# One pass instead of two over the second layer norm of an eight-core state-space and mixture-of-experts kernel

## What is computed

```python
def _layernorm(x, axis=-1, eps=1e-5):
    m = jnp.mean(x, axis=axis, keepdims=True)
    v = jnp.var(x, axis=axis, keepdims=True)
    return (x - m) / jnp.sqrt(v + eps)

x = L0_attn_x                                   # (4, 4096, 1024)
x = x + _L0_attn_ref(_layernorm(x), ...)        # a state-space scan per feature, then W_out
x = x + _L0_ffn_ref(_layernorm(x), ...)         # the second layer norm, router, 16 experts, shared MLP
return x
```

## Time and profile before

| what | us |
|---|---|
| median of the 2 timed runs | 9272.08 |
| the two runs | 8994.34 and 9549.82 |
| the profiled execution | 8383.0 |
| its span, core 2, the slowest | 8381.4 |
| spans of the 8 cores | 8336.9 to 8381.4 |
| TensorE busy in the span | 7658.5 (91%) |
| VectorE busy | 1614.3 (19%) |
| ScalarE busy | 662.4 (8%) |
| second layer norm, statistics pass | 1831.8 to 1879.4 |
| second layer norm, normalising pass | 1879.4 to 1930.8 |

### The profile page before, as it was taken

One profiled execution on the slowest core, in us unless ns is written; L12 is line 12 of the kernel. 1 busy time (PEld: TensorE's weight loads), 2 busy tenths in 40 slices (PEclk: granted clock), 3 DMA queues, 4 the chain that ended last, 5 costly groups with the idle time before them and its releaser, 6 DMA issues.

```text
span 8381.4 us, 128676 instructions; the slowest of 8 cores (8336.9 to 8381.4 us)
## 1 busy us (share of the span) xinstructions
PE 7658.5 (91%) x56312; PEld 6610.2 (79%) x56312; DVE 1614.3 (19%) x3078; ACT 662.4 (8%) x1195; POOL 479.2 (6%) x334
## 2 busy tenths in 40 slices
PE   0688888936999999999999997999999999999998
PEld 0688888424888888888888885888888888888886
DVE  5333333022111111111111111111111111111111
ACT  3211111011000000000000000000000000000000
POOL 0343433000000000000000000000000000000000
PEclk9655555967999999999999998999999999999998
DMA  2000000032011100110010102001110010100111
GB/s 81 15 3 3 3 3 5 20 123 66 31 36 45 41 31 31 51 41 31 31 49 33 41 31 71 31 31 35 46 41 31 31 51 31 41 31 31 51 41 41
DMA packets 129946, 309.18 MB, mean 37 GB/s; under 512 B 18384, under 2 KB 19408, under 8 KB 129392
## 3 DMA queue, kind: packets, MB, share of 16 engines
q1 hardware_dynamic: 124784, 284.17, 9.6%
q10 hardware_dynamic: 3456, 12.58, 0.5%
q0 software_dynamic: 1152, 4.19, 0.2%
HBM read 284.11 MB, written 16.78 MB: 36 GB/s over the span
## 4 chain that ended last, share of the span: by engine, by line
PE 88%; DVE 4%; POOL 2%; DMA 2%; issue 2%; ACT 1%; SPq 0%; DVEq 0%; POOLq 0%; ACTq 0%
PE ps L110 88%; POOL R L110 2%; DVE R L110 1%; ACT R L110 1%; DVE STA L110 1%; DMA SCA<-x1sp 1%; DVE SCB L110 1%; DMA SCA<-xo 1%; SPq L110 0%; DMA x1sp<-SCB 0%; DVE gsc L110 0%; DMA out<-SCB 0%; DVEq L110 0%; DVE hsb L110 0%; DMA R<-ws 0%
## 5 line engine op out<-in xcount | busy, mean ns | idle before, releaser
L110 PE MATMUL ps<-R 128*128 128x256 f32 (+3 forms) x33024 | 4976.8, 336 | 80.4 <-ACT R L110 33.3
L110 PEld LDWEIGHTS ps<-R 128*128 128x128 f32 (+1 forms) x33024 | 4330.8, 198 | 681.1 <-issue 169.3
L110 PE MATMUL ps<-SCA,R 128*128 128x256 f32 (+1 forms) x8704 | 1350.3, 328 | 4.8 <-DVE R L110 4.8
L110 PEld LDWEIGHTS ps<-SCA,R 128*128 128x128 f32 (+1 forms) x8704 | 1182.9, 200 | 135.2 <-issue 15.5
L110 PE MATMUL ps<-hsb,R 128*128 128x256 f32 x4608 | 1021.7, 382 | 0.0
L110 PEld LDWEIGHTS ps<-hsb,R 128*128 128x128 f32 x4608 | 878.9, 191 | 129.4 <-issue 9.3
L110 ACT ACTIVATE SCA<-ps,bcol 128x256 f32<-128x256 f32 x576 | 272.8, 474 | 5489.1 <-PE ps L110 5446.5
L110 DVE TENSOR_TENSOR R<-R,ps 128x256 f32<-128x256 f32 x1088 | 458.2, 421 | 953.3 <-PE ps L110 865.9
L110 PE MATMUL ps<-KE,R 128*128 128x128 f32 (+1 forms) x944 | 203.7, 396 | 468.7 <-POOL R L110 322.8
L110 PEld LDWEIGHTS ps<-KE,R 128*128 128x128 f32 (+1 forms) x944 | 174.6, 211 | 490.4 <-issue 490.3
L110 DVE SCALAR_TENSOR_TENSOR hsb<-ps,bcol,SCA 128x256 f32<-128x256 f32 x288 | 139.2, 483 | 2191.4 <-ACT SCA L110 2168.1
(11 more groups left out here) (74 smaller groups left out, 1573.7 us busy)
## 6 DMA issues: line engine op xcount, KB each, us to landing
R<-We SPq DMA_DIRECT2D x512, 256.0 KB, 5.3
R<-We SPq DMA_DIRECT2D x128, 512.0 KB, 5.2
SCA<-x1sp SPq DMA_DIRECT2D x40, 512.0 KB, 3.8
R<-ws SPq DMA_DIRECT2D x64, 256.0 KB, 6.4
x1sp<-SCB SPq DMA_DIRECT2D x16, 512.0 KB, 3.9
R<-ws SPq DMA_DIRECT2D x16, 512.0 KB, 8.0
out<-SCB SPq DMA_DIRECT2D x16, 512.0 KB, 2.9
SCA<-xo ACTq DMA_DIRECT2D x12, 512.0 KB, 4.6
```

The lines of the kernel that those rows point to most:

```text
L110: ins = getattr(e, attr)(*a, **kw)
```

## The change

The two passes are merged. For each pair of tiles the kernel loads both, takes their statistics, turns these into mean and reciprocal standard deviation with the small operations on two columns, and then normalises, transposes and copies both tiles from the same loaded data. Each tile of `x1sp` is loaded once. Even tiles are loaded from SyncE's program, odd ones from ScalarE's. A load of tile j waits until tile j-2 has been normalised. There are two landing places as before, and the squares go into the half of `SCB` that the normalised tile will overwrite.

```diff
-        x1d = []
-        for j in range(NT):
-            buf = SCA[:, (j % 2) * 1024:(j % 2) * 1024 + 1024]
-            if j == 0:
-                p.w(y, "dO", dO_x1)
-            if j < 2:
-                p.w(y, "sV", v_ev2[NT - 1])
-            if j >= 2:
-                p.w(y, "sS", sS3_0 + (j - 1))
-                p.w(y, "sV", sV3_0 + (j - 1))
-            x1d.append(p.dma(y, buf, x1sp[j * 128:(j + 1) * 128, :], "dX%d" % (j % 2)))
-        p.w(s, "dO", dO_x1)
-        for j in range(NT):
-            buf = SCA[:, (j % 2) * 1024:(j % 2) * 1024 + 1024]
-            p.w(s, "dX%d" % (j % 2), x1d[j])
-            p.inc(s.activation(SCB[:, 0:1024], buf, AF.Square,
-                               accum_out=STA[:, S_SUM3 + j:S_SUM3 + j + 1]), "sS")
-            p.w(v, "dX%d" % (j % 2), x1d[j])
-            p.inc(v.reduce_sum(STA[:, S_MU3 + j:S_MU3 + j + 1], buf, axis=AXX), "sV")
-        st16 = lambda c0_: STA[:, c0_:c0_ + 16]
...
-        sV_f3, sS_f3 = p.cnt["sV"], p.cnt["sS"]
-        for j in range(NT):
-            bufA = SCA[:, (j % 2) * 1024:(j % 2) * 1024 + 1024]
-            if j < 2:
-                p.w(y, "sV", sV_f3)
-                p.w(y, "sS", sS_f3)
-            if j >= 2:
-                p.w(y, "sV", vts_h[j - 2])
-            dj = p.dma(y, bufA, x1sp[j * 128:(j + 1) * 128, :], "dX%d" % (j % 2))
-            p.w(v, "dX%d" % (j % 2), dj)
-            p.w(v, "sV", vf3)
-            if j >= 2:
-                p.w(v, "sT", tx_h[j - 2])
-            bufB = SCB[:, (j % 2) * 1024:(j % 2) * 1024 + 1024]
-            vts = p.inc(v.tensor_scalar(bufB, bufA,
-                                        STA[:, S_MU3 + j:S_MU3 + j + 1],
-                                        STA[:, S_R33 + j:S_R33 + j + 1],
-                                        ALU.subtract, ALU.mult), "sV")
...
+        x1d = {}
+        for g0 in range(0, NT, 2):
+            for k in range(2):
+                j = g0 + k
+                bufA = SCA[:, (j % 2) * 1024:(j % 2) * 1024 + 1024]
+                qx = y if j % 2 == 0 else s
+                if j < 2:
+                    p.w(qx, "dO", dO_x1)
+                    p.w(qx, "sV", v_ev2[NT - 1])
+                else:
+                    p.w(qx, "sV", vts_h[j - 2])
+                x1d[j] = p.dma(qx, bufA, x1sp[j * 128:(j + 1) * 128, :],
+                               "dX%d" % (j % 2))
+            for k in range(2):
+                j = g0 + k
+                bufA = SCA[:, (j % 2) * 1024:(j % 2) * 1024 + 1024]
+                bufB = SCB[:, (j % 2) * 1024:(j % 2) * 1024 + 1024]
+                p.w(s, "dX%d" % (j % 2), x1d[j])
+                if g0 == 0 and k == 0:
+                    p.w(s, "dO", dO_x1)
+                p.inc(s.activation(bufB, bufA, AF.Square,
+                                   accum_out=STA[:, S_SUM3 + j:S_SUM3 + j + 1]), "sS")
+                p.w(v, "dX%d" % (j % 2), x1d[j])
+                p.inc(v.reduce_sum(STA[:, S_MU3 + j:S_MU3 + j + 1], bufA, axis=AXX),
+                      "sV")
+            stp = lambda c0_: STA[:, c0_ + g0:c0_ + g0 + 2]
+            p.w(v, "sS", p.cnt["sS"])
+            v.tensor_scalar_mul(stp(S_MU3), stp(S_MU3), 1.0 / D)
+            v.tensor_tensor(stp(S_R33), stp(S_MU3), stp(S_MU3), ALU.mult)
+            v.tensor_scalar_mul(stp(S_T0), stp(S_SUM3), 1.0 / D)
+            v.tensor_tensor(stp(S_R33), stp(S_T0), stp(S_R33), ALU.subtract)
+            v.tensor_scalar_add(stp(S_T0), stp(S_R33), EPS)
+            vx = p.inc(v.reciprocal(stp(S_T1), stp(S_T0)), "sV")
+            p.w(s, "sV", vx)
+            sx = p.inc(s.activation(stp(S_R33), stp(S_T1), AF.Sqrt), "sS")
+            p.w(v, "sS", sx)
+            v.tensor_tensor(stp(S_T2), stp(S_R33), stp(S_R33), ALU.mult)
+            v.tensor_tensor(stp(S_T2), stp(S_T0), stp(S_T2), ALU.mult)
+            v.tensor_scalar(stp(S_T2), stp(S_T2), -0.5, 1.5, ALU.mult, ALU.add)
+            p.inc(v.tensor_tensor(stp(S_R33), stp(S_R33), stp(S_T2), ALU.mult), "sV")
+            for k in range(2):
+                j = g0 + k
+                bufA = SCA[:, (j % 2) * 1024:(j % 2) * 1024 + 1024]
+                bufB = SCB[:, (j % 2) * 1024:(j % 2) * 1024 + 1024]
+                if j >= 2:
+                    p.w(v, "sT", tx_h[j - 2])
+                vts = p.inc(v.tensor_scalar(bufB, bufA,
+                                            STA[:, S_MU3 + j:S_MU3 + j + 1],
+                                            STA[:, S_R33 + j:S_R33 + j + 1],
+                                            ALU.subtract, ALU.mult), "sV")
+                vts_h.append(vts)
+                p.w(t, "sV", vts)
+                for hb in range(2):
+                    bank_i = 6 + hb
+                    bank_wait(bank_i)
+                    for kk in range(4):
+                        dcc = hb * 4 + kk
+                        src = bass.AP(SCB, (j % 2) * 1024 + dcc * 128,
+                                      [[2048, 128], [1, 128]])
+                        ins = t.matmul(PS[bank_i][:, kk * 128:(kk + 1) * 128], src,
+                                       KE[:, :], is_transpose=True, start=(kk == 0),
+                                       stop=(kk == 3), skip_group_check=True)
+                tx = p.inc(ins, "sT")
+                tx_h.append(tx)
+                p.w(s, "sT", tx)
+                for hb in range(2):
+                    dc0 = hb * 4
+                    ev = p.inc(s.copy(bass.AP(R1, dc0 * 2048 + j * 128,
+                                              [[16384, 128], [2048, 4], [1, 128]]),
+                                      PS[6 + hb][:, :]), "sS")
+                    bankfree[6 + hb] = ("sS", ev)
```

More of the change, by code:

```diff
@@ L820, in build_nc @@
-        for j in range(NT):
-            buf = SCA[:, (j % 2) * 1024:(j % 2) * 1024 + 1024]
-            p.w(s, "dX%d" % (j % 2), x1d[j])
-            p.inc(s.activation(SCB[:, 0:1024], buf, AF.Square,
-                               accum_out=STA[:, S_SUM3 + j:S_SUM3 + j + 1]), "sS")
-            p.w(v, "dX%d" % (j % 2), x1d[j])
-            p.inc(v.reduce_sum(STA[:, S_MU3 + j:S_MU3 + j + 1], buf, axis=AXX), "sV")
-        st16 = lambda c0_: STA[:, c0_:c0_ + 16]
-        p.w(v, "sS", p.cnt["sS"]); p.w(v, "sV", p.cnt["sV"])
```

## The result

The changed kernel took 1.0037 times as long as the kernel before, with a 95% interval of 1.0020 to 1.0053. On the profiled 8383 us that is 31 us, and the interval allows 17 to 44. The medians over all runs were 9065.11 us (43 runs, 8426.66 to 9631.67) and 8982.13 us (42 runs, 8375.49 to 9608.32). Executions of either kernel spread over 14 to 15%, because in many of them the cores of one half of the chip, or of both, are granted a lower TensorE clock, and the ratio compares only executions without that. What follows is read from the edited stage, where the granted clock is 0.50 on every core in every trace of these two kernels.

What follows compares the result with a forecast made beforehand. The second layer norm, 98.4 us with nothing beneath it, was bound by waits for loads, then transposes and copies. Head 11.3 + 7 x 15.4 + tail 7.2 = 126.3, so +28, +2 for weights, on 8383.0: 8413 us, range 8388 to 9580.

Steps and rivals of the forecast that it cites:

- the last line: Whole kernel: likeliest time 8413 us, range 8388 to 9580, beside two timed runs with a median of 9272.08.
- The sum: End time: profiled execution 8383.0 + 28 for the stage + 2 for late weights = 8413 us.
- head, first load to first normalising: Start of the second layer norm: first pair's load, sums, small operations and one table load, 11.3 us.
- one period: Merged loop, from normalising one even tile to that of the next pair: 15.4 us, taken seven times.
- place of the odd load in it: ScalarE issues the odd load behind the copies of the pair ahead, 6.71 us into the period.
- landing of a lone load: Odd load of a pair, from issue to landing: 4.0 us taken, 3.23 the shortest seen, 4.5 the upper bound.
- landing of the last load: Load 15 shares the DMA engines with the first expert's weights: +2 us taken, from +0.5 to +3.2.
- tail: End of the layer norm, from the last pair's normalising to its last copy: 6.64 + 0.59 = 7.2 us.
- Relief* rival: Edited stage: short landings, or a clock that rises within it; +5 to +17 us, about 8394; chance 0.09.
- table-load rival: Edited stage: each Sqrt, alternating with Square, loads its table; 9 us more, 8422; chance 0.05.
- rival of the vanished pass: Edited stage: statistics run beneath the pair ahead's transposes; period 10.5, gain of 6 us, 8377; chance 0.05.
- Slower than 2%: Expert loop: TensorE's clock comes back late after the longer stage; 8551 us or more; chance 0.03.

Runs made afterwards that it cites:

- e1: Changed kernel with the odd loads issued from SyncE instead of ScalarE; stage 109.4 to 110.5 us, ratio to the kernel before 1.001 (0.9966 to 1.0054).
- e3: Changed kernel with odd loads from SyncE and four landing places, each pair loaded a pair ahead; stage 109.4 to 110.8 us, period 13.0.
- e4: As e3, with the next pair's statistics ahead of this pair's copies and the odd tile in banks 4 and 5; stage 70.7 to 71.8 us, ratio 0.9927 (0.9807 to 1.0048).

## Right and wrong, by the steps of the prediction

**The time and range of the last line.** This is what was wrong. The change was forecast as +30 on the profiled 8383.0, and 8413 was written down beside a stated time before of 9272.08. Read against that number, 8413 is 9% faster, and the kernel became slower by 0.4%. The step that failed is the base, 8383.0 in "The sum": it is one execution at the short end of a spread of 14%. The prediction saw that the two timed runs lay 889 us higher and that no row explained it, and still took the profiled execution as its likeliest base. In its place the runs showed a median of 8982.13 for the kernel before, 599 above 8383.0, and no run of the changed kernel as short as 8413: its shortest took 8426.66, its median 9065.11. On the stated 9272.08 the same +30 would have read 9302. The range had been widened at the top to 9580 for that spread, so it held almost any execution of either kernel and said nothing of the change. A time that names its change, +30 on whatever base, would have been right.

**The sign and the size.** +30 was summed, +29 measured in the stage (127.5 against 98.4, and on the eight cores 128.1 against 99.5 in the mean), +31 by the ratio. The mechanism came as predicted: a serial period, an odd load behind the copies, an idle VectorE. The term list of the first trace, core 4, against the one predicted:

| term | predicted | measured |
|---|---|---|
| head, first load to first normalising | 11.3 | 1841.39 - 1829.42 = 12.0 |
| one period | 15.4 | (1929.59 - 1841.39) / 6 = 14.7 |
| place of the odd load in it | 6.71 | 6.99 |
| landing of a lone load | 4.0 | 3.2 to 3.4 |
| landing of the last load | 6.0 | 8.8 |
| tail | 7.2 | 1956.97 - 1949.73 = 7.2 |

**Mis-sized terms.** The landing was taken from loads that come in pairs; a lone one is as quick as the quickest of a busy chain. That made seven periods 5 us too long. The last load was priced at +2 over 4.0, between bounds of +0.5 and +3.2; over its neighbours it cost +5.5. Its row, was misread. In that stretch the loads of x1sp didn't run beside weights at all. ScalarE's last one was issued by 5163.6 and had landed when SyncE issued the first weight, in the timeline of core 2 of the kernel before:

```profile
5163.66 0.39 SPq L110 DMA_DIRECT2D SCA<-x1sp  x1
5170.86 5.05 SPq L110 DMA_DIRECT2D out<-SCB  x2
5176.00 12.11 SPq L110 DMA_DIRECT2D R<-ws  x20
```

So the 4.5 us is the price of a load beside one other load and a store. In the changed kernel eight weight transfers of 256 KB had been issued ahead of the last load (SyncE issued 11 in 6.07 us from 1932.30 on, the load went out at 1936.31), and no row of the prediction had that case.

The two errors cancel almost: -4.9 for the periods, +3.5 for the last load and +0.7 for the head bring the predicted 128.3 down to about 127.5. That the stage was met within 1 us is in part luck. The *Relief* rival had the short landing right and nothing else. The last load took most of it back, and the higher clock didn't come: eight transposes took 1.95 or 1.96 us in every pair of core 4, and the granted clock was 0.50 on all cores.

**The table-load rival fell.** The stage's table loads and its eight Sqrts, in the groups of ScalarE's instructions:

```profile
L110 ACT ACTIVATE STA<-STA 128x2 f32<-128x2 f32 x8 | 1.6, 203 | 13.4 <-DVE STA L110 13.4
L110 ACT ACT_TABLE_LOAD x1 | 1.3, 1283 | 2.1 <-DVE STA L110 2.1
```

One load for eight alternations of Square and Sqrt, as the earlier trace rows had it.

**The rival of the vanished pass** decides below a period of 11.4. With the program's order it isn't reached: 14.7, and 13.0 with the load in time (e1, e3), the very figure that was set against it. With another order it is, 7.6 (e4). So the rival failed for the reason given, the Squares behind the copies, as far as e3 and e4 tell: e4 changed the banks as well.

**Slower than 2%** did not happen. The router's stretch had a clock of 0.76 after the longer stage on core 4, and 0.73 on the core of the earlier trace rows.

## What to carry to other kernels

Before two passes are merged, write down the chain through one round of the merged loop: removing half of the loads gained nothing here, because two passes that each overlapped became one that didn't. In a loop with few buffers, issue the transfers from a program that has nothing else to wait for; a DMA issue, or a Square for the next round, that stands behind this round's copies is late by all of them. And state a predicted change together with the base it is added to.

## What was not expected of the hardware

**The clock ahead of the stage.** On some cores the granted clock of the product with `Wout` was lower, in the same execution: columns as in the first fence, core 6 of the changed kernel's first trace:

```profile
1480.00:1725.00 245.00, 232.36 (x506) 103.25 (x505) 16.45 (x24) 17.19 (x25) 0.00 (x0) 0.81 0.05 17
```

and core 4 of the same trace:

```profile
1480.00:1725.00 245.00, 230.74 (x595) 105.90 (x595) 15.91 (x23) 21.31 (x31) 0.00 (x0) 1.00 0.06 17
```

Core 6 did 506 matmuls in the time of core 4's 595, and its layer norm began at 1882 instead of 1829. That is 53 us, more than the change moved. In this trace cores 0, 1, 6 and 7 had it. Their router's stretch also took 120 to 122 us at a clock of 0.69 or 0.70, against 112 to 115 on the others, and their expert loop had 0.81 against 0.92. In the second trace of the changed kernel cores 0 and 1 had 0.81 in the product too, but then 113 and 114 us in the router's stretch and 0.98 in the loop. In seven of the twelve traces one or two pairs of neighbouring cores had 0.80 to 0.82 in the product, all three of the changed kernel among them; in the one trace of the kernel before none had. The code of that stage is the same in all of them but the two of the kernel with x1 kept, where only what follows it differs. What decides it stays open.

**A hundredth of clock is worth more than the change.** Within one execution of the changed kernel the spans of the cores went with the mean granted clock: 8440.8 us at 0.891 and 8338.0 at 0.904, 103 us for 0.013. A difference of 30 us can only be read from the stage itself, or from many runs.
